# Four banks of the next projection moved to either side of the output's turn and of the norm's averages, with VectorE's and ScalarE's steps for them

## What is computed

```python
# layer 0: attention over the 4096 positions of each image
q = prelu(conv1x1(gn(x), w1, b1), a1)      # 24 channels
k = prelu(conv1x1(gn(x), w2, b2), a2)      # 24 channels
v = prelu(conv1x1(gn(x), wa, ba), aa)      # 192 channels
x = x + softmax(q.T @ k) @ v
# layer 1: for each channel a chain 1 -> 3 -> 3 -> 3 -> 1 of small
# matrices with tanh gates, of gn(x) - 0.5 and of gn(x) + 0.5
x = x + max(|sigmoid(s*upper) - sigmoid(s*lower)|, 1e-6)
```

## Time and profile before

| | |
|---|---|
| three runs, median (lowest to highest) | 4864.96 us (4863.04 to 4870.57) |
| span of the profiled execution | 4866.3 us |
| TensorE busy, share of the span | 4460.5 us, 92% |
| VectorE busy | 4178.8 us, 86% |
| ScalarE busy | 3717.8 us, 76% |
| GpSimd busy | 937.5 us, 19% |
| mean granted clock of TensorE | 0.982 |

### The profile page before, as it was taken

How to read it: one execution, slowest core, us unless ns; L and a number is a source line. 1 busy time by engine, 2 the same in 40 slices (tenths; PEclk the granted TensorE clock), 3 DMA queues, 4 the chain that set the end, 5 groups by cost and what they waited for, 6 DMA issues and landing times.

```text
span 4866.3 us, 107519 instructions
## 1 busy us (share of the span) xinstructions
PE 4460.5 (92%) x38780; PEld 2978.2 (61%) x38780; DVE 4178.8 (86%) x5433; ACT 3717.8 (76%) x4214; POOL 937.5 (19%) x937
## 2 busy tenths in 40 slices
PE   6999989999899998999899998999989999899976
PEld 4888347773477725777257762678617785277821
DVE  6897899978999798996999969899698987989866
ACT  2776887768877697776977769777797777977787
POOL 4200202212122111221112120121202212022112
PEclk9999999999999999999999999999999999999988
DMA  2001421114211142111412023120332113311133
GB/s 66 25 20 30 100 70 47 34 39 105 62 47 40 36 110 51 47 40 46 108 45 57 28 62 98 39 58 27 77 86 60 36 38 73 96 42 34 38 88 95
DMA packets 154989, 279.95 MB, mean 58 GB/s; under 512 B 37441, under 2 KB 37921, under 8 KB 152706
## 3 DMA queue, kind: packets, MB, share of 16 engines
q1 hardware_dynamic: 154434, 272.69, 21.8%
HBM read 205.24 MB, written 50.33 MB: 53 GB/s over the span
## 4 chain that ended last, share of the span: by engine, by line
PE 57%; DVE 17%; issue 13%; ACT 12%; DMA 1%; DVEq 0%; ACTq 0%; SPq 0%; POOL 0%; POOLq 0%
PE ps L1486 10%; PE ps L1488 10%; PE ps L1490 10%; PE ps L1261 7%; DVE mxp L1164 6%; PE ps L1438 6%; ACT th L777 5%; ACT arena L770 5%; DVE arena L1058 4%; PE ps L1360 3%; PE ps L1294 3%; DVE th L1096 3%; PE ps L1346 3%; PE ps L1318 2%; PE ps L1253 1%
## 5 line engine op out<-in xcount | busy, mean ns | idle before, releaser
L1486 PE MATMUL ps<-v_sb,arena 128*128 128x193 f16 x8192 | 2017.5, 246 | 18.4 <-DVE arena L1058 18.4
L1488 PE MATMUL ps<-v_sb,arena 128*128 128x192 f16 x8192 | 2026.6, 247 | 0.0
L1490 PE MATMUL ps<-v_sb,arena 128*128 128x193 f16 x8192 | 2009.6, 245 | 0.0
L732 ACT ACTIVATE arena<-ps 128x1024 f16<-128x1024 f32 x1024 | 1049.9, 1025 | 773.8 <-PE ps L1261 772.8
L1058 DVE TENSOR_TENSOR arena<-arena 128x1024 f16<-128x1024 f32 x1024 | 1346.1, 1316 | 258.4 <-ACT arena L735 258.3
L1164 DVE TENSOR_REDUCE mxp<-ps 128x1 f32<-128x512 f32 x1792 | 1162.2, 683 | 32.5 <-PE ps L1438 24.8
L1096 DVE SCALAR_TENSOR_TENSOR th<-th,gates,ps 128x1024 f32<-128x1024 f32 x768 | 949.9, 1275 | 148.7 <-ACT th L777 141.4
L735 ACT ACTIVATE arena<-ps 128x1024 f32<-128x1024 f32 x1024 | 1046.4, 1022 | 0.2 <-DVE arena L1058 0.2
L1488 PEld LDWEIGHTS ps<-v_sb,arena 128*128 128x128 f16 x8192 | 794.8, 97 | 261.8 <-issue 0.3
L777 ACT ACTIVATE th<-ps,biases 128x1024 f32<-128x1024 f32 x768 | 826.1, 1120 | 119.9 <-PE ps L1346 81.5
L1486 PEld LDWEIGHTS ps<-v_sb,arena 128*128 128x128 f16 x8192 | 792.0, 97 | 150.5 <-issue 28.6
(11 more groups left out here) (147 smaller groups left out, 3448.3 us busy)
## 6 DMA issues: line engine op xcount, KB each, us to landing
x<-x2d SPq DMA_DIRECT2D x1152, 64.0 KB, 2.4
arena<-x2d SPq DMA_DIRECT2D x768, 64.0 KB, 2.5
xp<-x_dram SPq DMA_DIRECT2D x18, 1536.0 KB, 10.1
shared<-x_dram SPq DMA_DIRECT2D x64, 384.0 KB, 3.7
x2d<-shared SPq DMA_DIRECT2D x64, 384.0 KB, 3.0
res<-x2d SPq DMA_DIRECT2D x96, 256.0 KB
out_dram<-res SPq DMA_DIRECT2D x96, 256.0 KB
kst<-shared SPq DMA_DIRECT2D x32, 256.0 KB, 3.3
```

Source lines behind the costliest of these rows:

```text
L732: act.activation(e_hi[:, q % 4, :].rearrange("p (k n) -> p k n", k=2), sc, ACT.Exp)
L1486: pe.matmul(acc, eh, v_sb[:, m, 0:C + 1], start=(m == 0 and t % 2 == 0), stop=False, skip_group_check=True)
L1488: pe.matmul(acc[:, 0:C], eh, v_sb[:, m, VW:VW + C], start=False, stop=False, skip_group_check=True)
L1490: ins = pe.matmul(acc, el, v_sb[:, m, 0:C + 1], start=False, stop=(m == MT - 1), skip_group_check=True)
```

## The change

On TensorE bank 1 goes ahead of the output's turn, bank 2 between the turn and the first averages, bank 3 between the two averages, bank 4 between the second averages and the spread of the norm. On ScalarE four negative parts instead of three stand ahead of the wait for `biases` (AHEAD), and all later ones move one place forward. On VectorE `value(2)` goes between `own` and `statc`, and `low_part(1)` directly behind `w1s`. No work is added or taken away, and nothing changes in crossing 8.

```diff
+AHEAD = 4
@@ ScalarE, phase_a
                 normalise(l, BLOCKS - 1)
                 if proj:
-                    for n in range(3):
+                    for n in range(AHEAD):
                         negative(n)
                 act.wait_ge(gn2_step, l * GN2_STEPS + 16)
                 for i in range(LEAD):
                     first_tanh(i)
                     if proj:
-                        negative(3 + i)
+                        negative(AHEAD + i)
                 if proj:
-                    for n in range(3 + LEAD, QK + V_LEAD):
+                    for n in range(AHEAD + LEAD, QK + V_LEAD):
                         negative(n)
@@ VectorE, phase_a
                 if proj:
                     low_part(0)
                 next(chain2)
+                if proj:
+                    value(2)
                 next(chain2)
                 if proj:
-                    for n in range(2, QK + V_LEAD):
+                    low_part(1)
+                    for n in range(3, QK + V_LEAD):
                         query(n)
@@ TensorE, phase_a
+                if proj:
+                    qk_bank(1)
                 pe.wait_ge(out_norm, l * BLOCKS + BLOCKS + START)
                 pe.wait_ge(x2_ready, l * 2 * BLOCKS + 2 * BLOCKS - 2 + START)
                 for h in range(2):
                     turn_out(BLOCKS - 1, h)
                 if proj:
-                    qk_bank(1)
+                    qk_bank(2)
                 averages2(l, 0)
+                if proj:
+                    qk_bank(3)
                 averages2(l, 1)
                 if proj:
-                    qk_bank(2)
+                    qk_bank(4)
                 pe.wait_ge(gn2_step, l * GN2_STEPS + 12)
                 pe.matmul(ps[:, 6, 0:4 * PER_H], sel_sb[:, 0:P], own.rearrange("p q k -> p (q k)"), start=True,
                           stop=True).then_inc(gn2_mm, 1)
                 if proj:
-                    for n in range(3, QK):
+                    for n in range(5, QK):
                         qk_bank(n)
```

## The result

Seven runs of the changed kernel have a median of 4881.11 us (4876.98 to 4882.29), seven of the kernel before 4868.23 us (4863.04 to 4870.57). The ratio is 1.0026 with a 95% interval of 1.0015 to 1.0037: **slower by 0.26%**, some 13 us. The profiled execution has a span of 4879.3 us against 4866.3.

What follows compares the result with a forecast made beforehand. The start of bank 10 was taken to set a crossing's worth. 4866.3 us, less 6.7 gained, plus 15.4 lost to late half clock, gave 4875.0; 1.3 less for the runs' median gave 4873.7 us, range 4857 to 4882.

Steps and rivals of the forecast that it cites:

- likeliest case: Full clock through the norm's chain, half clock around the start of bank 10; 4869 to 4881 us, chance 0.66.
- sign of being wrong: Clock at 1.00 throughout banks 10 to 12, or at 0.50 already in banks 2 to 4, would refute the prediction.
- late loss: At banks 10 to 12: half clock after a TensorE gap of 3.3 us, 2.2 us a crossing, +15.4 us together.
- Step 1: Bank 1 ahead of the turn waits for the loop's taken branch, so the add comes 1.66 us late.
- Steps 3 and 4: Banks 3 and 4 around the second averages: at full clock bank 3 costs 0.1 us, bank 4 is free.
- third rival: Clock also falls early, around the turn, as transposes do not count as busy; 4893 us, chance 0.06.
- Step 5: At the norm's spread, `statc` comes 0.90 us behind the start of `own`; it and the first tanh are 0.61 us late.
- Crossing 5: First tanh at 2872.24 against 2872.41, since half clock had delayed even the first averages before; gain 1.67 us.
- Step 6: One negative part moved ahead of the tanhs: bank 10 starts 11.83 us behind the first tanh, 1.50 us earlier than 13.33.

Runs made afterwards that it cites:

- the 22 in the late pause: The changed kernel with 22 unused fp32 transposes ahead of bank 10, where TensorE idles: 4861.74 us, ratio 0.9992.
- work in the pause: The changed kernel with three unused matmuls between value banks 9 and 10, where TensorE idles 3.17 us: 4865.21 us, ratio 0.9989.
- TensorE's order alone: The kernel before with only TensorE's new order, ScalarE and VectorE as before: 4890.81 us, ratio 1.0042.

## Why the prediction was right

The forecast was 4873.7 us with a range of 4857 to 4882; 4881.11 us lies at its upper end. Its likeliest case, kept through the norm and lost at bank 10, is what happened in crossings 3, 4, 6 and 7; in 1, 2 and 5 the clock fell early too, which the prediction had named as a sign of being wrong (0.50 in banks 2 to 4, crossings 1 and 2). I gave slower 0.35 and same 0.58, with the bound 1 us above the forecast. Of the 7.4 us that were missing, 3.3 are the level of the kernel before, whose median of three runs was 4864.96 us and of seven 4868.23; the sum was some 4 us short. That it was no further off is in part luck: the first tanhs were 6.2 us dearer than forecast, the late loss 4.2 us cheaper, and 2.4 us came between the crossings.

- **Step 1, the branch.** Right. The add of crossing 3 comes 5.60 us behind bank 0 instead of 4.02: 1.58 late, 1.66 forecast. Bank 1 back behind the turn takes all of it away. The Trainium skill's 108 ns for a compare-and-branch (Advanced Engine Details and Errata, Control Flow Timing) would by the prediction's estimate have made the turn 0.2 us late; the trace has 1.62.
- **Steps 3 and 4, "if the clock is full".** Right in crossings 3, 4, 6 and 7. In crossings 1 and 2 the clock fell in bank 3, behind the pause of 1.36 us ahead of the first averages, and the second averages came 1.5 and 3.4 us late against the kernel before. In outcome this is in part the third rival. Its mechanism, transposes that the clock does not count, is not borne out by the 22 in the late pause; at the turn itself it was not tested. Why the clock fell in these crossings and not in the others, with the same pauses or longer ones, is open. The place of bank 1 seems to have to do with it: in the four kernels with TensorE's new order and bank 1 ahead of the turn the clock fell before the first tanh in 10 of 28 crossings (changed 1, 2, 5; work in the pause 4, 5; TensorE's order alone 4, 5, 7; transposes 1, 7), in the four with bank 1 behind it in none of 28.
- **Step 5, mis-sized.** In crossings 2 to 7 `statc` follows `own` by 1.04 us, not 0.90: `value(2)` starts 0.19 us behind the end of `own`. The first tanh follows `statc` by 1.38 instead of 1.10, a term that the sum did not have: `shifted` takes 0.54 instead of 0.24 us while GpSimd casts what `value(2)` gave it. Together with the branch the first tanh of crossing 3 is 0.96 late (4, 6 and 7: 1.00 to 1.04) where 0.61 was forecast. In crossing 1 it is 2.49 late instead of 0.95 and in crossing 2 it is 2.70 late instead of 0.61, with the early fall.
- **Crossing 5, mis-sized.** I had its first tanh 0.17 us early; it came 0.83 late, since its clock had fallen ahead of the turn, in bank 1.
- **Step 6.** Right to 0.02 us: 11.82 to 11.83 behind the first tanh. TensorE's order alone leaves 13.34.
- **The late loss, mis-sized.** 11.2 us instead of 15.4. The forecast had the clock fall from 0.6 us before to 1.5 us behind the start of bank 10. In crossings 3, 4, 6 and 7 it fell 1.8 to 2.1 us before it, for 6.83 us, and cost 2.03 to 2.18 us; in 2 and 5 it fell 0.5 to 0.6 us behind it, for 3.41 us, and cost 1.39; in crossing 1, where the early stretch had lasted to 495.15, TensorE had a pause of 2.51 us and the clock held. The forecast also took 3.41 us for a stretch in which TensorE is busy throughout; the earlier trace rows has one of 6.83 us busy throughout, and here crossing 1 has one of 10.24. Windows of the changed kernel, the stretch of crossing 1 and the early and the late one of crossing 2:

```profile
484.91:495.15 10.24, 10.24 (x16) 4.41 (x15) 7.36 (x21) 4.48 (x5) 2.24 (x4) 0.50 0.15 44
1082.24:1085.65 3.41, 3.41 (x7) 1.30 (x6) 1.35 (x5) 0.00 (x0) 0.62 (x1) 0.50 0.44 120
1102.72:1106.13 3.41, 3.41 (x12) 3.41 (x12) 1.24 (x3) 0.49 (x1) 2.81 (x5) 0.50 0.42 115
```

| term, us, seven crossings | forecast | measured |
|---|---|---|
| first tanh later | +3.8 | +10.0 |
| first tanh to bank 10 | -10.5 | -10.6 |
| late loss | +15.4 | +11.2 |
| sum at the first layer | +8.7 | +10.6 |

The profiled spans differ by 13.0 us. The 2.4 us that this leaves lie between the crossings, a term that the sum did not have: the six stretches from a first layer to the next bank 0 take 3.7 us more in all, since the clock falls in every one of them and before it held in three, and what follows the last crossing takes 1.2 us less.

## What to carry to other kernels

Filling an engine's idle time ahead of a bound can move the idle time instead of removing it (here to 3.17 us ahead of bank 10): ask where the engine will run out of work instead, and whether something stands on the chain there. TensorE's clock makes this a matter of the whole path: keeping it early in the kernel before won 9.0 us ahead of the first tanhs and lost 15.2 us behind them. A useless matmul in a pause is a quick test for such a loss. Work put at the head of a loop's body is not free before the branch is through: the turn behind it came 1.62 us late. And where two kernels differ by some 5 us, look at the stretches that were not edited too; here they alone differ by up to 11.5 us between two kernels.

## What was not expected of the hardware

- Two matmuls added to idle time made the kernel before slower by 0.17% (0.08 to 0.26%), by way of the clock 17 us further on.
- 22 transposes in the pause hold the clock as three matmuls do (4861.74 and 4865.21 us; 4.47 us for the 24 matmuls in both). The Trainium skill (TensorE: Matmul & The Clock Gate, Part 4) says that a transpose does not count as busy for the clock in the same way, beside its measurement of bf16 ones; these fp32 ones did as well as matmuls.
- In the changed kernel the clock fell right behind a pause of 1.36 us in crossings 1 and 2, and not in 3, 4, 6 and 7 with the same pause.
- A step of 0.24 us on VectorE (`shifted`) takes 0.54 us while GpSimd runs a cast beside it (1685.57 to 1686.23), and 0.24 us again with `value(2)`, and so the cast, moved away.
- In crossing 1 of the kernel before with two matmuls more the clock fell after three pauses of 0.22, 0.94 and 0.53 us, none of them long. What decides a fall is not settled by these runs.
